# Moving three pieces of work in a hand-ordered attention slot: O's codes on ScalarE, the attention rest and the lower half of Q's weights on VectorE

## The chip, the cores and the metric

The kernel runs on one core of a Trainium2 chip. The metric is the device time of one execution in microseconds (us), lower is better. TensorE does the matrix products, VectorE, ScalarE and GpSimd the rest, and the SyncE queue issues most of the transfers. Every engine works its instructions off in the order in which the program gives them to it, and they meet at semaphores only.

## The reference

One decoder layer in float32 with x of shape (2, 512, 1024):

```python
# 1. self attention, 4-bit weights: (codes - 8) * scale of each 128 rows
h = layernorm(x); q, k, v = h @ Wq, h @ Wk, h @ Wv     # 32 query heads, 8 key/value heads of 128
q, k = rope(q), rope(k)
attn = softmax(q @ k.T / sqrt(128) + causal mask)
x = x + (attn @ v) @ Wo
# 2. cross product with quantised operands
x = x + fake_quant(layernorm(x)) @ fake_quant(ctx)
# 3. dense layer with binarised weights
x = x + layernorm(x) @ binarize(weight).T
```

## The kernel before

The work on attention is cut into 64 **slots**, one for each pair of a query head and a batch element (p = 0 to 63, the batch element b is p mod 2, so even slots are batch 0 and odd ones batch 1). Eight slots make a group (one key/value head for both batch elements). Group 0 is written out, groups 1 to 4 (slots 8 to 39) are a loop of the hardware, in which each slot also prepares a piece of ctx on ScalarE and GpSimd, and groups 5 to 7 are written out again. In slots 0 to 6 and from 41 on the slots also turn pieces of the dense weight.

Each engine has its own list of a slot's work, written by hand (functions `slot`):

- **TensorE**, slot p: `scores(p,0)` (L839 to L841), the last unit of the O product of the slot before, `o_unit(p-1,3)` (L876), `scores(p,1)`, `o_unit(p,0)`, one eighth of the Q projection for slot p+2 (`q_part`, L699 to L701), `scores(p,2)`, more of Q, `o_unit(p,1)`, the rest of Q, `o_unit(p,2)`, and `weigh(p-1)` (L856), attention times V of the slot before, into the PSUM bank `pv_ps`.
- **ScalarE**, slot p: the exponentials of the three score units (`exps`, L1195), the upper half of q (L1187), `q_cut` (L1106), `prob_split(p,0)` (L1222), the two halves of the swap for RoPE (`q_swap`, L1111 and L1112), `ao_part(p-1)` (L1231, the upper half of attention's output, out of `pv_ps`), `prob_split(p,1)` and `o_cut` (L1208, O's codes from int32 to float16). In the loop the parts of ctx stand between (L1289, L1301, L1316) and one load is issued (L1276).
- **VectorE**, slot p: in odd slots a small copy of O's scales (`o_scales`, L1976), `maxima(p,0)` (L1966), `q_sum(p+1)` (L1895, RoPE's last sum), the O add of unit 3 of the slot before (`o_add`, L1990), `maxima(p,1)`, `o_add(p,0)`, `maxima(p,2)`, reciprocals (L2063, L2067) with `piece_scale` (L1722) between them, `piece_lo` (L1728, the lower half of Q's weights), `o_add(p,1)`, `o_add(p,2)`, `q_cos` (L1885) and `ao_rest(p-1)` (L2006, the lower half of attention's output, out of `pv_ps`).
- **GpSimd**, slot p: the lower half of q (L1541), the normalisation (L1527), the clip of ctx (L1635), the lower half of the probabilities (L1534), and between its two parts `sine` (L1522), which `q_sum` waits for.

Waits that matter here: `scores(p,2)` waits for the first exponentials of its slot, which wait for `maxima(p,0)`. The first Q eighth of a slot waits for `q_sum`. And `o_unit` has this wait, in which `cb` is 0 in odd slots and 4 in even ones (`unit_of`):

```python
if k == 0:
    pe.wait_ge(o_codes_done, p - 2)
    if cb == 0:
        pe.wait_ge(ao_ready, p - 1)
```

`ao_ready` counts the `ao_rest` that are done, so that an odd slot's first O unit needs `ao_rest(0)` to `ao_rest(p-2)`.

Of the kernel before, what the change touches and what calls it, by code (L numbers as in the profile page):

```python
# [51 lines left out]
SLOTS = B * RF  # L52
# [70 lines left out]
def wf_late(p):  # L123

    if p < KB:
        return p
    return p - WF_FROM + KB - 1 if p > WF_FROM else None


def wf_early(p):  # L130

    if p < KB:
        return p + 1 if p + 1 < KB else None
    return p - WF_FROM + KB if p >= WF_FROM else None
# [67 lines left out]
def build(nc, x_in, ctx_in, codes, scales, q_scales, q_scalars, ffn_w, rope_cos, rope_sin, ident_in, mask_in, out):  # L202
    with ExitStack() as ctx:
# [303 lines left out]
        def known(n):  # L507
            return isinstance(n, int)
# [580 lines left out]
        def _(act):  # L1089
# [126 lines left out]
            def prob_split(p, part):  # L1216

                act.wait_ge(norm_done, p * 2 + (part + 1))
                if part == 0 and not (known(p) and p == 0):
                    act.wait_ge(prob_turned, p * TURNED)  # L1220
                for at, to, w in prob_runs(part):
                    ins = act.activation(prob16[:, 0, to:to + w], prob[:, at:at + w], ACT.Copy)  # L1222
                ins.then_inc(prob_hi[part], 1)
# [25 lines left out]
            def wf_sign(u):  # L1249

                raw, diff = wf_place(u)
                act.wait_ge(wf_clipped, u + 1)
                if u >= 2:
                    act.wait_ge(wf_split, u)
                act.activation(diff, raw, ACT.Sign).then_inc(wf_signed, 1)
# [8 lines left out]
            def slot(g, i, with_ctx=False):  # L1264
                p = g * SLOTS + i
                has_prev = not (known(p) and p == 0)
                has_next = not (known(p) and p >= N_SLOTS - 1)
                has_ahead = not (known(p) and p >= N_SLOTS - Q_AHEAD)
                has_piece = not (known(p) and p + FIRST_PIECES >= N_CUT)

                if with_ctx:
                    q, dst = ctx_half(g, i)

                    tile = ctx_rows[bass.ds((g - 1) * 4 + i // 2, 1), :, (i % 2) * S:(i % 2 + 1) * S]
                    act.wait_ge(ctx_free, q + 1)
                    act.dma_start(ctx_raw[:, :], tile.rearrange("a p n -> (a p) n")).then_inc(ctx_landed, 16)  # L1276
                if known(p) and p == 1:
                    late_swaps()
                if known(p) and p == 2:
                    late_upper()  # L1280
                exps(p, i, 0)
                if has_next:
                    q_hi(p + 1)
                exps(p, i, 1)
                if known(p) and wf_late(p) is not None:
                    wf_upper(wf_late(p))
                if with_ctx:
                    act.wait_ge(ctx_landed, q * 16 + 16)
                    act.activation(ctx_raw[:, :], ctx_raw[:, :], ACT.Identity, scale=scal[:, 5:6],  # L1289
                                   bias=scal[:, 3:4]).then_inc(ctx_scaled, 1)  # L1290
                exps(p, i, 2)
                if has_piece:
                    q_cut(p, i)
                if known(p) and 0 < p < O_LAG:
                    v_evict(V_HERE + p - 1)
                if known(p) and wf_early(p) is not None:
                    wf_sign(wf_early(p))
                prob_split(p, 0)
                if with_ctx:
                    act.wait_ge(ctx_clipped, q + 1)  # L1300
                    act.activation(ctx_raw[:, :], ctx_raw[:, :], ACT.Copy, bias=ROUND).then_inc(ctx_rounded, 1)  # L1301
                if has_ahead:
                    q_swap(p + Q_AHEAD)
                if known(p) and p == N_SLOTS - 1:
                    prob_split(p, 1)
                    o_cut(p, i)
                    column_part(0, 0)
                    ao_part(p - 1, i - 1)
                    return
                if has_prev:  # L1310
                    ao_part(p - 1, (i - 1) % SLOTS)
                prob_split(p, 1)
                o_cut(p, i)
                if with_ctx:
                    act.wait_ge(ctx_rounded, q + 1)
                    act.activation(dst, ctx_raw[:, :], ACT.Copy, bias=-(ROUND + Q_MID)).then_inc(ctx_free, 1)  # L1316
# [364 lines left out]
        def _(dve):  # L1681
# [234 lines left out]
            def wf_lower(u):  # L1916

                dve.wait_ge(wf_hi, u + 1)
                dve.scalar_tensor_tensor(wf_halves[:, 1, :], wf_place(u)[1], F_UP, wf_halves[:, 0, :],
                                         ALU.mult, ALU.subtract).then_inc(wf_split, 1)  # L1920
# [89 lines left out]
            def slot(g, i):  # L2010
                p = g * SLOTS + i
                has_prev = not (known(p) and p == 0)
                has_next = not (known(p) and p >= N_SLOTS - 1)
                has_ahead = not (known(p) and p >= N_SLOTS - Q_AHEAD)
                has_o = not (known(p) and p < O_LAG)
                has_piece = not (known(p) and p + FIRST_PIECES >= N_CUT)
                n = p + FIRST_PIECES

                if known(p) and p == N_SLOTS - 1:
                    j = o_scales(g, i)  # L2020
                    maxima(p, i, 0)
                    o_add(p - 1, i - 1, 3)
                    maxima(p, i, 1)
                    dve.wait_ge(o_now_ready, j)
                    o_add(p, i, 0)
                    maxima(p, i, 2)
                    dve.wait_ge(exp_done, p * 3 + 2)
                    dve.reciprocal(row_inv[:, 0:3], row_sum[:, 0:3]).then_inc(inv_ready[0], 1)
                    dve.wait_ge(exp_done, p * 3 + 3)
                    dve.reciprocal(row_inv[:, 3:4], row_sum[:, 3:4]).then_inc(inv_ready[1], 1)  # L2030
                    wf_lower(wf_late(p))
                    j = o_scales(g, i, NH)
                    o_add(p, i, 1)
                    wf_difference(wf_early(p))
                    o_add(p, i, 2)
                    o_add(p, i, 3)
                    ao_rest(p - 1, i - 1)
                    for k in range(UNITS):
                        o_add(N_SLOTS, 0, k)
                    dve.wait_ge(o_now_ready, j)  # L2040
                    return
                if has_o and i % B:
                    j = o_scales(g, i)
                if i or known(p):
                    maxima(p, i, 0)
                if known(p) and p == 0:
                    wf_difference(0)
                if has_next:
                    q_sum(p + 1)
                if not (i or known(p)):  # L2050
                    maxima(p, i, 0)
                if has_o and not (known(p) and p == O_LAG):
                    o_add(p - 1, (i - 1) % SLOTS, 3)
                maxima(p, i, 1)
                if has_o:
                    if i % B:
                        dve.wait_ge(o_now_ready, j)
                    o_add(p, i, 0)
                maxima(p, i, 2)
                if known(p) and p < 3:  # L2060
                    (late_join, late_sum, late_lower)[p]()
                dve.wait_ge(exp_done, p * 3 + 2)
                dve.reciprocal(row_inv[:, 0:3], row_sum[:, 0:3]).then_inc(inv_ready[0], 1)  # L2063
                if has_piece:
                    piece_scale(n, i % 2)
                dve.wait_ge(exp_done, p * 3 + 3)
                dve.reciprocal(row_inv[:, 3:4], row_sum[:, 3:4]).then_inc(inv_ready[1], 1)  # L2067
                if known(p) and wf_late(p) is not None:
                    wf_lower(wf_late(p))
                if has_piece:  # L2070
                    piece_lo(n, i % 2, q_region(i), Q_UP)
                if has_o:
                    o_add(p, i, 1)
                if known(p) and wf_early(p) is not None:
                    wf_difference(wf_early(p))
                if has_o:
                    o_add(p, i, 2)
                if known(p) and 0 < p < O_LAG:
                    v_rest(V_HERE + p - 1)
                if has_ahead:  # L2080
                    q_cos(p + Q_AHEAD)
                if has_prev:
                    ao_rest(p - 1, (i - 1) % SLOTS)

            def body(g, with_ctx=False):
                for i in range(SLOTS):
# [186 lines left out]
```

## Time and profile before

| what | value |
|---|---|
| time, median of 3 runs | 1104.35 us (1102.6 to 1105.29) |
| span of the profiled execution, first to last instruction | 1104.9 us |
| granted TensorE clock, mean | 0.992 |
| TensorE busy | 1056.7 us, 96% |
| VectorE busy | 934.1 us, 85% |
| ScalarE busy | 690.9 us, 63% |
| GpSimd busy | 689.6 us, 62% |

The profile is one execution. Times of rows are microseconds from the start of its span. No other device time is given for the profiled execution; its span is 0.55 us above the median of the runs. "PEld" is TensorE's loading of weights, which runs beside its products.

### The profile page before, as it was taken

The page shows a single profiled execution, that of the slowest core. Times are in us where ns is not written, and L with a number is a line of the kernel's source. Part 1 is how long each engine was busy: PE and PEld are TensorE (multiplying, and loading weights), DVE is VectorE, ACT ScalarE, POOL GpSimd, SP SyncE. Part 2 cuts the span into 40 slices and gives each one's busy share as a digit, 9 for nine tenths or more (in the row PEclk, how much of TensorE's full clock was granted, in tenths as well). Part 3 has the DMA queues.
Part 4 walks back from the last instruction along what each step waited for, and adds up shares of the span by engine and source line. Part 5 has one row for each costly group of instructions (what it writes and reads, how often), then busy time and mean ns, then how long its engine had stood idle before and what let it go on. Part 6 is the DMA issues. An engine that isn't in the chain of part 4 may idle for free.

```text
span 1104.9 us, 18938 instructions
## 1 busy us (share of the span) xinstructions
PE 1056.7 (96%) x5448; PEld 513.8 (47%) x5448; DVE 934.1 (85%) x1755; ACT 690.9 (63%) x1502; POOL 689.6 (62%) x770
## 2 busy tenths in 40 slices
PE   3898999899999999999999999999999999989998
PEld 2443444444544444444444444544544544444443
DVE  7977897799888888888888889999999998888873
ACT  4455665766777777777777776666666666463320
POOL 2457546877767766776777677777878777332200
PEclk9999999999999999999999999999999999999999
DMA  9344231767678667657766765777777675432453
GB/s 350 123 135 132 67 101 44 150 149 170 142 155 160 145 147 159 159 134 154 163 148 141 159 160 130 148 155 162 151 150 171 142 128 119 108 117 53 101 103 79
DMA packets 301204, 153.65 MB, mean 139 GB/s; under 512 B 249264, under 2 KB 261808, under 8 KB 301136
## 3 DMA queue, kind: packets, MB, share of 16 engines
q1 hardware_dynamic: 293360, 139.46, 55.3%
q10 hardware_dynamic: 7776, 13.37, 4.4%
q8 instruction: 32, 0.52, 0.2%
q14 instruction: 36, 0.29, 0.1%
HBM read 89.07 MB, written 4.19 MB: 84 GB/s over the span
## 4 chain that ended last, share of the span: by engine, by line
PE 78%; DVE 8%; ACT 5%; POOL 3%; issue 3%; ACTq 1%; DMA 1%; SPq 1%; DVEq 0%; POOLq 0%
PE side_ps L699 10%; PE side_ps L856 9%; PE side_ps L701 9%; PE side_ps L700 9%; PE proj_ps L876 8%; PE out_ps L876 8%; PE proj_ps L1027 4%; PE score_ps L839 3%; PE score_ps L841 2%; PE score_ps L840 2%; PE proj_ps L1032 2%; PE score_ps L998 2%; PE out_ps L719 2%; PE score_ps L719 2%; PE proj_ps L699 2%
## 5 line engine op out<-in xcount | busy, mean ns | idle before, releaser
L1534 POOL TENSOR_TENSOR w_b<-prob,w_b 128x896 f16<-128x896 f32 (+2 forms) x192 | 188.9, 998 | 30.6 <-ACT w_b L1222 30.0
L699 PE MATMUL side_ps<-hT,w_a 128*128 128x512 f16 x504 | 191.1, 379 | 1.5 <-DVE rot L1895 1.5
L701 PE MATMUL side_ps<-hT,w_a 128*128 128x512 f16 x504 | 191.0, 379 | 0.0
L700 PE MATMUL side_ps<-hT,w_a 128*128 128x512 f16 x504 | 191.0, 379 | 0.0
L1990 DVE SCALAR_TENSOR_TENSOR x_acc<-proj_ps,o_now,x_acc 128x1024 f32<-128x1024 f32 x120 | 153.6, 1280 | 37.8 <-PE proj_ps L876 37.8
L1527 POOL TENSOR_SCALAR prob<-prob,row_inv 128x512 f32<-128x512 f32 (+3 forms) x256 | 170.7, 681 | 22.6 <-DVE row_inv L2063 16.9
L1195 ACT ACTIVATE prob<-score_ps,neg_max 128x512 f32<-128x512 f32 (+3 forms) x256 | 132.9, 521 | 47.4 <-DVE neg_max L1966 38.6
L1541 POOL TENSOR_TENSOR q_sb<-rot,q_sb 128x512 f16<-128x512 f32 x64 | 75.0, 1172 | 139.8 <-ACT q_sb L1187 139.8
L1990 DVE SCALAR_TENSOR_TENSOR x_acc<-out_ps,o_now,x_acc 128x1024 f32<-128x1024 f32 x120 | 152.7, 1272 | 0.0
L876 PE MATMUL proj_ps<-work,w_b 128*128 128x512 f16 x496 | 127.3, 379 | 1.9 <-DVE x_acc L1990 1.1
L876 PE MATMUL out_ps<-work,w_b 128*128 128x512 f16 x496 | 127.3, 379 | 1.3 <-DVE x_acc L1990 1.2
L1966 DVE CUSTOM_DVE_ANT_0 score_ps<-score_ps,mask_b 128x512 f32<-128x512 f32 (+3 forms) x256 | 122.1, 497 | 2.0 <-PE score_ps L841 2.0
L1222 ACT ACTIVATE w_b<-prob 128x896 f16<-128x896 f32 (+2 forms) x192 | 99.5, 553 | 34.2 <-POOL prob L1527 30.2
L856 PE MATMUL side_ps<-work,v_sb 128*128 128x512 f16 (+3 forms) x768 | 116.0, 301 | 1.3 <-DMA work<-w_b 1.3
L1522 POOL TENSOR_TENSOR swapped<-swapped,sin_t 128x512 f32<-128x512 f32 x79 | 101.8, 1288 | 22.0 <-ACT swapped L1112 21.8
L856 PEld LDWEIGHTS side_ps<-work,v_sb 128*128 128x128 f16 (+1 forms) x768 | 70.2, 99 | 46.6 <-DMA work<-w_b 1.8
L1231 ACT ACTIVATE work<-side_ps 128x512 f16<-128x512 f32 x64 | 38.2, 597 | 73.1 <-PE side_ps L856 73.0
L839 PE MATMUL score_ps<-k_sb,q_sb 128*128 (+4 forms) x256 | 77.2, 302 | 3.3 <-ACT prob L1195 2.1
L699 PEld LDWEIGHTS side_ps<-hT,w_a 128*128 128x128 f16 x504 | 49.2, 98 | 65.5 <-issue 10.6
L1187 ACT ACTIVATE q_sb<-rot 128x512 f16<-128x512 f32 x64 | 40.3, 630 | 58.9 <-PE score_ps L841 57.6
L701 PEld LDWEIGHTS side_ps<-hT,w_a 128*128 128x128 f16 x504 | 49.3, 98 | 59.5
L840 PE MATMUL score_ps<-k_sb,q_sb 128*128 (+4 forms) x256 | 76.8, 300 | 0.0
(238 smaller groups left out, 2102.5 us busy)
## 6 DMA issues: line engine op xcount, KB each, us to landing
stage_c<-in_codes_dram SPq DMA_DIRECT2D x80, 256.0 KB, 2.9
stage_o<-in_codes_dram SPq DMA_DIRECT2D x64, 256.0 KB, 3.9
stage_s<-in_scales_dram SPq DMA_DIRECT2D x64, 256.0 KB, 3.8
ctx_raw<-in_ctx_dram ACTq DMA_DIRECT2D x32, 256.0 KB, 3.2
work<-w_b SPq DMA_TRANSPOSE x261, 3.0
x_acc<-in_x_dram SPq DMA_DIRECT2D x8, 512.0 KB, 8.5
k_sb<-in_codes_dram SPq DMA_DIRECT2D x16, 256.0 KB, 6.4
v_sb<-in_scales_dram SPq DMA_DIRECT2D x16, 256.0 KB, 7.3
```

Of the source, the lines that this page charges most:

```text
L699: pe.matmul(o, stat(0), mov(0), start=first, stop=False)
L700: pe.matmul(o, stat(0), mov(1), start=False, stop=False)
L701: return pe.matmul(o, stat(1), mov(0), start=False, stop=last)
L839: pe.matmul(o, q[0], k[0], start=True, stop=False)
L856: mm = pe.matmul(pv_ps[:, kb * P:S], v_sb[:, bass.ds(g, 1), l, b * TB + kb, :].rearrange("p a d -> p (a d)"), probT[:, m, at:kb + (TB - 1) ...
L876: mm = pe.matmul(o[:, b, :], o_codes[:, h % RING, cb * P:(cb + 1) * P], ao[:, h % 2, l, b * S:(b + 1) * S], start=l == 0, stop=l == 1)
L1195: ins = act.activation(prob[:, SCORE_AT[qb]:SCORE_AT[qb] + w], score_ps[:, score_bank(i, u), off:off + w], ACT.Exp, bias=neg_max[:, c:c + ...
L1522: pool.tensor_tensor(swapped[:, :], swapped[:, :], sin_t[:, :], ALU.mult).then_inc(done, 1)
L1527: return pool.tensor_scalar(prob[:, at:at + w], prob[:, at:at + w], row_inv[:, col:col + 1], P_UP, ALU.mult, ALU.mult)
L1534: ins = pool.tensor_tensor(prob16[:, 1, to:to + w], prob[:, at:at + w], prob16[:, 0, to:to + w], ALU.subtract)
L1966: ins = dve.tensor_tensor_reduce(s, s, mask_b[:, S - w:S], -1.0, MAX_FROM, ALU.add, ALU.min, neg_max[:, c:c + 1])
L1990: ins = dve.scalar_tensor_tensor(y, u, s, y, ALU.mult, ALU.add)
```

## The change

On ScalarE `o_cut` moves from behind `prob_split(p,1)` to ahead of `prob_split(p,0)`. On VectorE `ao_rest(p-1)` leaves the end of slot p and stands in slot p+1, behind `maxima(p+1,0)` and `q_sum(p+2)` and ahead of the first O add. `piece_lo` moves from ahead of `o_add(p,1)` to behind it. Nothing is added or taken away, and the lists of TensorE, GpSimd and SyncE are the same.

```diff
@@ ScalarE, slot
                     wf_sign(wf_early(p))
+                o_cut(p, i)
                 prob_split(p, 0)
...
                 prob_split(p, 1)
-                o_cut(p, i)
@@ VectorE, slot
+                has_before = not (known(p) and p < 2)
                 if known(p) and p == N_SLOTS - 1:
                     j = o_scales(g, i)
                     maxima(p, i, 0)
+                    ao_rest(p - 2, i - 2)
                     o_add(p - 1, i - 1, 3)
...
                 if not (i or known(p)):
                     maxima(p, i, 0)
+                if has_before:
+                    ao_rest(p - 2, (i - 2) % SLOTS)
                 if has_o and not (known(p) and p == O_LAG):
                     o_add(p - 1, (i - 1) % SLOTS, 3)
...
+                if has_o:
+                    o_add(p, i, 1)
                 if has_piece:
                     piece_lo(n, i % 2, q_region(i), Q_UP)
-                if has_o:
-                    o_add(p, i, 1)
...
                     q_cos(p + Q_AHEAD)
-                if has_prev:
-                    ao_rest(p - 1, (i - 1) % SLOTS)
```

## Rows read from the trace of the kernel before

**Rows 1.** The page: busy time by engine, and the chain that ended last.
```profile
PE 1056.7 (96%) x5448; PEld 513.8 (47%) x5448; DVE 934.1 (85%) x1755; ACT 690.9 (63%) x1502; POOL 689.6 (62%) x770
...
PE 78%; DVE 8%; ACT 5%; POOL 3%; issue 3%; ACTq 1%; DMA 1%; SPq 1%; DVEq 0%; POOLq 0%
```

**Rows 2.** Waits from 240 to 980 us: total, times, longest.
```profile
PEld score_ps L839 <- ACT prob L1195: 16.8, 33, 0.9
...
PEld side_ps L699 <- DVE rot L1895: 6.6, 16, 0.5
```

**Rows 3.** Timeline of TensorE, odd slot 37: start, duration, line, operation.
```profile
629.29 0.38 PE L839 MATMUL score_ps<-k_sb,q_sb 128*128 x1
...
629.72 0.38 PE L841 MATMUL score_ps<-k_sb,q_sb 128*128 x1
...
631.46 1.03 PE L876 MATMUL proj_ps<-work,w_b 128*128 128x512 f16 x4
...
633.13 0.28 PE L839 MATMUL score_ps<-k_sb,q_sb 128*128 x1
```

**Rows 4.** Timeline of VectorE, the same stretch.
```profile
630.12 0.69 DVE L2006 SCALAR_TENSOR_TENSOR work<-side_ps,work 128x512 f16<-128x512 f32 x1 [0.36 <-ACT work L1231]
630.73 0.39 DVE L1976 COPY o_now<-work 128x8 f32 x1
631.04 0.68 DVE L1966 CUSTOM_DVE_ANT_0 score_ps<-score_ps,mask_b 128x512 f32<-128x512 f32 x1
...
631.65 0.68 DVE L1895 TENSOR_TENSOR rot<-side_ps,swapped 128x512 f32<-128x512 f32 x1
632.25 1.27 DVE L1990 SCALAR_TENSOR_TENSOR x_acc<-out_ps,o_now,x_acc 128x1024 f32<-128x1024 f32 x1
```

**Rows 5.** Timeline of ScalarE, slots 36 and 37.
```profile
630.49 0.62 ACT L1208 ACTIVATE w_b<-stage_o 128x512 f16<-128x512 int32 x1
...
632.88 0.19 ACT L1195 ACTIVATION_READ_ACCUMULATOR prob<-score_ps,neg_max 128x1 f32 x1
...
637.68 0.95 ACT L1222 ACTIVATE w_b<-prob 128x896 f16<-128x896 f32 x1 [0.57 <-POOL prob L1527]
```

**Rows 6.** Timeline of GpSimd, the same stretch.
```profile
629.03 1.27 POOL L1522 TENSOR_TENSOR swapped<-swapped,sin_t 128x512 f32<-128x512 f32 x1
630.67 0.43 POOL L1534 TENSOR_TENSOR w_b<-prob,w_b 128x128 f16<-128x128 f32 x1 [0.37 <-ACT w_b L1222]
```

**Rows 7.** Timeline of TensorE: starts of the even slots 36 and 38.
```profile
617.12 0.38 PE L839 MATMUL score_ps<-k_sb,q_sb 128*128 x1
...
641.36 0.38 PE L839 MATMUL score_ps<-k_sb,q_sb 128*128 x1
```

**Rows 8.** Timeline: starts of slots 57, 58 and 59, and slot 57's sine.
```profile
869.44 0.38 PE L839 MATMUL score_ps<-k_sb,q_sb 128*128 128x512 f16 x1
...
881.48 0.38 PE L839 MATMUL score_ps<-k_sb,q_sb 128*128 128x512 f16 x1
...
893.38 0.38 PE L839 MATMUL score_ps<-k_sb,q_sb 128*128 128x512 f16 x1
...
869.13 1.27 POOL L1522 TENSOR_TENSOR swapped<-swapped,sin_t 128x512 f32<-128x512 f32 x1
```

**Rows 9.** Timeline of TensorE, VectorE and GpSimd, slot 3.
```profile
218.49 1.02 PE L876 MATMUL proj_ps<-work,w_b 128*128 128x512 f16 x4 [0.84 <-issue]
220.39 0.38 PE L699 MATMUL side_ps<-hT,w_a 128*128 128x512 f16 x1 [0.88 <-DVE rot L1895]
...
218.31 0.74 DVE L1976 COPY o_now<-work 128x8 f32<-128x8 f32 x1
...
217.75 1.27 POOL L1522 TENSOR_TENSOR swapped<-swapped,sin_t 128x512 f32<-128x512 f32 x1
```

**Rows 10.** Timeline of TensorE, slots 1 and 41.
```profile
197.36 0.28 PE L839 MATMUL score_ps<-k_sb,q_sb 128*128 128x256 f16 x1 [1.11 <-ACT prob L1195]
...
681.29 0.38 PE L699 MATMUL side_ps<-hT,w_a 128*128 128x512 f16 x1 [0.62 <-DVE rot L1895]
```

More of the change, by code:

```diff
@@ L1312, in slot @@
                 prob_split(p, 1)
-                o_cut(p, i)
                 if with_ctx:
```

## The prediction

> **What bounds the kernel now.** I read the page first: TensorE is busy for 96% of the span and carries 78% of the chain that ended last [rows 1]. So a change of order can only give back TensorE's gaps, or make new ones. The list of waits says which gaps the attention slots have: the third score unit waits for the first exponentials, and the first eighth of Q waits for RoPE's sum on VectorE [rows 2]. Then I read the timeline of one pair of slots, engine by engine, to see the size. In the loop the even slot 36 takes 12.17 us (617.12 to 629.29) and the odd slot 37 takes 12.07 us (629.29 to 641.36) [rows 3, 7]. Behind the loop an even slot without a gap takes 11.90 us (slot 58) and an odd one 12.04 us (slot 57) [rows 8]. TensorE's list is the same in all of them, so I take 11.90 us as the slot that has no gap. A pair has 0.44 us of gaps in the loop and 0.14 us behind it. These are all that the change can win in the steady part.
>
> **Why the gaps are there.** I count from W, the start of `scores(p,0)`, 629.29 in slot 37. Its last product ends at 630.10 (W+0.81) [rows 3]. The first maximum could start some 0.04 us later; that step between engines is an estimate, from TensorE's 0.06 us behind the exponentials' end below. It starts at 631.04 (W+1.75), because `ao_rest` (630.12) and the copy of the scales (630.73) stand ahead of it [rows 4]. The exponentials follow, their sum is read out by 633.07 (632.88 and 0.19), and TensorE starts the third score unit at 633.13 [rows 3, 5]. ScalarE is late too: it has O's codes at 630.49 (0.62 us) between its splits and the exponentials [rows 5].
>
> **The change, part by part.**
>
> *O's codes ahead of the split.* ScalarE stands idle for 0.57 us ahead of `prob_split(p,0)`, waiting for GpSimd [rows 5]. The 0.62 us of `o_cut` lie in that hole, up to 0.05 us of them perhaps not. Its own waits are long met there: its codes were loaded a slot earlier, and the O units that it waits for are done by `scores(p,1)`. If that cover were gone it would put 0.62 us ahead of the swaps, and they are `q_cos`'s wait. No transfer moves: SyncE sees `o_codes_done` in the next slot. Behind, ScalarE is free about 0.5 us earlier, so in the loop the exponentials end at about 632.57 instead of 633.07, W+3.3; the third score unit wants them at W+3.68 (633.13, W+3.84, less the odd slot's gaps of 0.17 us). That gap closes.
>
> *`piece_lo` behind the second O add.* O add 2 waits for its unit on TensorE after both, so the pair ends as before. `piece_done` comes 1.2 us later, but SyncE reads it only behind the turns of the slot, and TensorE only in the next slot. I cost it at nothing. What covers it is VectorE's wait ahead of O add 2; without that it would be at most the move itself, one O add of 1.27 us [rows 4], and then `q_cos` and the next maximum would be late.
>
> *`ao_rest` behind the next slot's first maximum.* In an even slot nobody wants it soon, and the maximum starts about 0.6 us earlier. The gaps go. In an odd slot TensorE wants it: `o_unit(p,0)` has the wait on `ao_ready` for `ao_rest(p-2)`, which is now in the same slot. The unit starts at 631.46, W+2.17, with `ao_rest` done at 630.81, 0.65 us before [rows 3, 4]. Afterwards VectorE has the maximum, `q_sum` and only then `ao_rest`. From one start to the next these take 0.61 us (631.04 to 631.65) and 0.60 us (631.65 to 632.25), then `ao_rest` takes 0.69 us, and I add 0.05 us until TensorE starts [rows 4]. That is 1.95 us from the maximum's start. With the maximum at W+0.85 TensorE starts its unit at W+2.80 and stands still for 0.63 us. Everything behind it in TensorE's list stands with it: Q's eighth, `scores(p,2)` and, through them, ScalarE's upper half of q. That a wait of this kind is real can be seen in slot 3: there the O unit starts at 218.49, after TensorE stood still for 0.84 us, and VectorE left `ao_rest` for the copy at 218.31 [rows 9].
>
> *The copy of the scales.* It moves up with the maximum, to about W+0.4, and there GpSimd is in its `sine` (629.03 to 630.30) [rows 6]. Two rows say what that does. In slot 37 the copy starts 0.06 us after a GpSimd TENSOR_TENSOR that ends at 631.10, and ends at 631.12 [rows 4, 6]. In slot 3 it starts inside `sine`, which ends at 219.02, takes 0.74 us for 8 elements, and ends at 219.05 [rows 9]. So the copy ends 0.03 us after the GpSimd instruction, and the maximum starts 0.09 us before the copy's end. The Trainium skill (SBUF — State Buffer, "SBUF: two separate sides") has the rule for it: the port pair that VectorE and GpSimd share is an exclusive lock for a whole instruction, whichever starts first. By that rule the copy waits for all of `sine`; if the copy were free, the stall would be the 0.63 us above.
>
> When does `sine` end? In slot 37 at W+1.01. Its chain starts from the reciprocals of the even slot before, and that slot gets 0.27 us shorter on TensorE while GpSimd's work does not: W+1.28, less some 0.03 us by which the reciprocals come earlier, so W+1.25. The maximum then starts at 1.25+0.03-0.09, W+1.19, and the stall is 1.19+1.95-2.17 = 0.97 us. Behind the loop the even slot has no gap to lose: `sine` ends at 870.40, W+0.96 in slot 57 [rows 8], the maximum starts at W+0.90, and the stall is 0.68 us.
>
> **The sum.** In the loop, 16 odd slots by 0.97 us = 15.5 us. Slots 41 to 61, 11 odd ones by 0.68 us = 7.5 us. Slots 5 and 7, 1.4 us. Slot 3: its copy ends at 219.05 as before, the maximum starts at 218.96, `ao_rest` ends 1.90 us later, and the O unit starts at 220.91 and not at 218.49; Q's eighth, which now starts at 220.39, starts at 221.77: 1.4 us more. Slot 1: its third score unit waited 1.11 us for exponentials on ScalarE [rows 10]; `o_cut` is out of that chain, 0.5 us less. The end of slot 63: 0.1 us more, for one `ao_rest` ahead of its O adds. Together 25.4 us. Against it stand the gaps that go: 16 pairs by 0.44 us = 7.0 us, 10 odd slots behind the loop by 0.14 us = 1.4 us and the 0.62 us of slot 41 [rows 10], and 0.3 us in slots 5 and 7: 9.3 us. Net 16.1 us on the profiled execution's span of 1104.9 us, so 1121.0 us; the median of the runs is 0.55 us lower, and I predict 1120.4 us, 1.5% slower.
>
> **The rivals.**
>
> *The copy doesn't wait (or hardly).* The same stall, but 0.63 us each: 29 odd slots give 18.3 us, slot 3 less its copy's wait 0.7 us, less 0.4 and 9.3 us: +9.3 us, 1113.7 us. For it: other copies fell into a short GpSimd instruction, so I have only slot 3 for a long one. Against it: both rows end with the GpSimd instruction to 0.03 us.
>
> *The stall doesn't bite, and the change is faster.* One mechanism: `ao_rest` is done by W+2.1, so that only the gaps go: 1104.35-9.3-0.5 = 1094.6 us. It decides at a stall of 9.8 us over 30 odd slots, 0.33 us each: below that the kernel gets faster. For it: TensorE has other work ahead, 0.65 us of slack. Against it: three VectorE instructions of known length stand between score and `ao_rest`, and even the short count is 0.3 us over that point. *No measurable change* lies around that point, 1101 to 1107.7 us; 0.3% is about what a measurement of this kernel can tell from no change.
>
> *The exponentials stay late.* The maximum comes earlier but ScalarE, with its load and ctx work, does not start them earlier: the even slots of the loop keep 0.27 us, 16 of them 4.3 us, 1124.7 us. The same price would come if `piece_lo`, which reads two SBUF tiles, or `wf_difference` behind it ran into GpSimd's long TENSOR_TENSOR and O add 2 came late. Against it: 0.4 us of room by the count above.
>
> **How the numbers follow.** The forecast has 0.60, the copy that doesn't wait 0.17, the late exponentials 0.07, no change 0.07, and faster 0.09. Slower by over 0.3% is the first three, 0.84. The bounds of the forecast's own stall are 0.63 and 1.1 us in the loop (the copy free, and `sine` 0.1 us later than counted), from 1114 to 1124 us with the rest. For 8 in 10 the range reaches down over the copy's rival and up over the late exponentials: 1109 to 1126 us.
>
> **What would show it.** In odd slots TensorE's first O unit starts behind L2006's end, at about W+3.1 in the loop and W+2.85 behind it, and the list of waits gets a line of some 20 us, L876 on L2006. The copy L1976 ends with L1522. The third score unit waits for exponentials nowhere in the loop, and even slots take 11.90 us, odd ones about 12.87 us. If the copies last 0.16 to 0.39 us and odd slots 12.5 us, the rival of the free copy is right. If odd slots stay below 12.2 us, the wait was hidden and my count from the maximum to `ao_rest` is wrong.

## The result, and the profile after

| | before | after |
|---|---|---|
| time, median (4 runs each) | 1104.82 us (1102.6 to 1105.6) | 1126.85 us (1124.69 to 1127.37) |
| span of the profiled execution | 1104.9 us | 1125.5 us |
| granted TensorE clock, mean | 0.992 | 0.991 |

The ratio is 1.0200, with a 95% interval of 1.0187 to 1.0214: 2.0% slower, 22.0 us between the medians. 1120.4 us was forecast, so the direction and the place were right, and 6.45 us are missing; the time lies 0.85 us above the range.

The page of the kernel after, busy time by engine and the chain that ended last:
```profile
PE 1054.1 (94%) x5448; PEld 519.5 (46%) x5448; DVE 945.9 (84%) x1755; ACT 683.2 (61%) x1502; POOL 680.4 (60%) x770
...
PE 76%; DVE 12%; issue 5%; POOL 3%; ACT 2%; DMA 1%; DVEq 0%; SPq 0%; ACTq 0%; POOLq 0%
```
Against [rows 1] TensorE's work is the same (2.6 us less busy), and its share of the chain fell from 78% to 76%. VectorE's rose from 8% to 12%: more of the chain now runs over VectorE. The waits from 240 to 980 us, total, times and longest:
```profile
ACT q_sb L1187 <- PE score_ps L841: 102.9, 58, 2.5
...
PEld proj_ps L876 <- issue: 31.1, 30, 1.6
PE proj_ps L876 <- DVE work L2005: 15.6, 16, 1.1
...
PE proj_ps L876 <- issue: 10.8, 14, 1.5
```
The third score unit's wait for the exponentials [rows 2] is no longer among the long ones. In its place TensorE waits at the O unit: 16 times for VectorE's L2005, `ao_rest`, in the loop's 16 odd slots, and 14 times "issue" (no releaser found) in those of the written-out groups, 26.4 us together. ScalarE's wait for `scores(p,2)` ahead of the upper half of q doubled, from 51.8 to 102.9 us; it stands behind the same stall, as forecast.

The odd slot 37, where W is 640.46. TensorE (the first product of each kind), then VectorE, then GpSimd (start, duration, line, operation, idle time before):
```profile
640.46 0.38 PE L839 MATMUL score_ps<-k_sb,q_sb 128*128 x1
...
642.57 0.22 PE L841 MATMUL score_ps<-k_sb,q_sb 128*128 x1
643.73 1.03 PE L876 MATMUL proj_ps<-work,w_b 128*128 128x512 f16 x4 [0.95 <-DVE work L2005]
...
645.25 0.27 PE L839 MATMUL score_ps<-k_sb,q_sb 128*128 x1
...
653.47 0.38 PE L839 MATMUL score_ps<-k_sb,q_sb 128*128 x1
```
```profile
640.83 0.86 DVE L1975 COPY o_now<-work 128x8 f32 x1
641.60 0.69 DVE L1965 CUSTOM_DVE_ANT_0 score_ps<-score_ps,mask_b 128x512 f32<-128x512 f32 x1
...
642.21 0.68 DVE L1894 TENSOR_TENSOR rot<-side_ps,swapped 128x512 f32<-128x512 f32 x1
642.82 0.67 DVE L2005 SCALAR_TENSOR_TENSOR work<-side_ps,work 128x512 f16<-128x512 f32 x1
643.41 1.27 DVE L1989 SCALAR_TENSOR_TENSOR x_acc<-out_ps,o_now,x_acc 128x1024 f32<-128x1024 f32 x1
```
```profile
638.55 1.88 POOL L1533 TENSOR_TENSOR w_b<-prob,w_b 128x896 f16<-128x896 f32 x1
640.40 1.26 POOL L1521 TENSOR_TENSOR swapped<-swapped,sin_t 128x512 f32<-128x512 f32 x1
```
The stall can be followed from right to left. The O unit, at W+2.17 before [rows 3], starts at W+3.27, 0.24 us after `ao_rest` ends (643.49). Ahead of `ao_rest` stand the sum and the maximum, 0.61 us each. The maximum starts at W+1.14, 0.09 us before the end of a copy of 8 elements that takes 0.86 us and ends 0.03 us after `sine`. The third score unit follows without a wait, and the next slot starts after 13.01 us instead of 12.07.

Behind the loop, slot 57 (W 887.76), TensorE, VectorE and GpSimd:
```profile
890.76 0.81 PE L876 MATMUL proj_ps<-work,w_b 128*128 128x512 f16 x3 [0.68 <-issue]
```
```profile
888.13 0.73 DVE L1975 COPY o_now<-work 128x8 f32<-128x8 f32 x1
888.77 0.69 DVE L1965 CUSTOM_DVE_ANT_0 score_ps<-score_ps,mask_b 128x512 f32<-128x512 f32 x1
...
889.99 0.67 DVE L2005 SCALAR_TENSOR_TENSOR work<-side_ps,work 128x512 f16<-128x512 f32 x1
```
```profile
887.56 1.27 POOL L1521 TENSOR_TENSOR swapped<-swapped,sin_t 128x512 f32<-128x512 f32 x1
```
`sine` ends at W+1.07, the maximum starts at W+1.01, and the step from `ao_rest`'s end (890.66) to TensorE is 0.10 us. The O unit is at W+3.00.

In ScalarE's list of slot 37 the second edit shows:
```profile
649.05 0.62 ACT L1208 ACTIVATE w_b<-stage_o 128x512 f16<-128x512 int32 x1
649.67 0.95 ACT L1222 ACTIVATE w_b<-prob 128x896 f16<-128x896 f32 x1
```
The split follows `o_cut` with no idle time; the hole of 0.57 us [rows 5] is filled.

The span in stretches, from one start of `scores(p,0)` to another (us), each worked out as a difference of two starts in TensorE's timeline (the first and the last from the span's start and to its end):

| stretch | before | after | difference | forecast |
|---|---|---|---|---|
| up to slot 0 | 181.87 | 180.88 | -1.0 | 0 |
| slots 0 to 2 | 34.32 | 33.80 | -0.5 | -0.5 |
| slot 3 | 13.06 | 15.50 | +2.4 | +1.4 |
| slots 4 to 7 | 47.87 | 49.25 | +1.4 | +1.1 |
| slots 8 to 39 | 388.47 | 398.98 | +10.5 | +8.5 |
| slots 40 to 61 | 263.76 | 271.33 | +7.6 | +5.5 |
| from slot 62 on | 175.55 | 175.76 | +0.2 | +0.1 |
| span | 1104.9 | 1125.5 | +20.6 | +16.1 |

In the loop even slots went from 12.19 to 11.90 us and odd ones from 12.09 to 13.04 (means of 16).

### The profile page after: what moved, and what is told of

The parts are those of the page before. It is cut to its first block, busy times and chain, and to the rows that moved or that the text cites. A ratio compares the mean times of both kernels' runs of the same rounds, so it can differ in the third digit from the quotient of the medians.

```text
span 1125.5 us, 18942 instructions
## 1 busy us (share of the span) xinstructions
PE 1054.1 (94%) x5448; PEld 519.5 (46%) x5448; DVE 945.9 (84%) x1755; ACT 683.2 (61%) x1502; POOL 680.4 (60%) x770
## 4 chain that ended last, share of the span: by engine, by line
PE 76%; DVE 12%; issue 5%; POOL 3%; ACT 2%; DMA 1%; DVEq 0%; SPq 0%; ACTq 0%; POOLq 0%
PE proj_ps L876 10%; PE side_ps L701 9%; PE side_ps L700 9%; PE side_ps L699 9%; PE out_ps L876 8%; PE side_ps L856 7%; PE proj_ps L1027 4%; PE score_ps L839 2%; PE score_ps L841 2%; PE score_ps L840 2%; PE proj_ps L1032 2%; PE score_ps L998 2%; PE proj_ps L699 1%; PE proj_ps L700 1%; PE proj_ps L701 1%
## 5 line engine op out<-in xcount | busy, mean ns | idle before, releaser
L1526 POOL TENSOR_SCALAR prob<-prob,row_inv 128x512 f32<-128x512 f32 (+3 forms) x256 | 170.4, 678 | 19.4 <-DVE row_inv L2066 12.8
L876 PEld LDWEIGHTS proj_ps<-work,w_b 128*128 128x128 f16 x496 | 44.8, 98 | 80.0 <-issue 34.6
L701 PEld LDWEIGHTS side_ps<-hT,w_a 128*128 128x128 f16 x504 | 49.4, 98 | 59.6 <-issue 0.3
```

The costliest lines, as they stand in the source:

```text
L701: return pe.matmul(o, stat(1), mov(0), start=False, stop=last)
L876: mm = pe.matmul(o[:, b, :], o_codes[:, h % RING, cb * P:(cb + 1) * P], ao[:, h % 2, l, b * S:(b + 1) * S], start=l == 0, stop=l == 1)
L1526: return pool.tensor_scalar(prob[:, at:at + w], prob[:, at:at + w], row_inv[:, col:col + 1], P_UP, ALU.mult, ALU.mult)
```

## The experiments

All times are medians, with lowest and highest. The kernel before was run beside them, 9 times with e1 to e4 and 13 times with e5 to e8, and has 1104.68 us both times. Lengths of slots are from one profiled execution of each kernel.

### e1: the attention rest alone

`ao_rest` moved; `o_cut` and `piece_lo` where they were.
```diff
-                o_cut(p, i)                 # ScalarE, ahead of prob_split(p, 0)
...
                 prob_split(p, 1)
+                o_cut(p, i)
...
+                    piece_lo(n, i % 2, q_region(i), Q_UP)
                 if has_o:
                     o_add(p, i, 1)
-                if has_piece:
-                    piece_lo(n, i % 2, q_region(i), Q_UP)
```
Expected: 

> Only the attention rest moves; O's codes and the lower half of Q's weights stay where they were. My theory (the odd slot's first O unit waits for the attention rest): all of the loss is here, and the loop's even slots keep their 0.27 us gap because ScalarE still has O's codes ahead of the exponentials, 16 x 0.27 = 4.3 us and 0.5 us in slot 1 more than the whole change: about 1131.5 us, odd slots of the loop near 13.0 us, even ones 12.1 to 12.2 us. Rival (the loss comes from the other two moves running into GpSimd or the swaps): near 1105 us.

Measured: 1128.18 us (1126.17 to 1130.21), ratio 1.0215 (1.0201 to 1.0229). This one move is the whole loss. The even slots kept their 12.19 us; the list of waits has what is left of the late exponentials, and the timeline of slot 37 (W 640.95) has a shorter hold:
```profile
PEld score_ps L839 <- ACT prob L1195: 9.5, 15, 0.9
```
```profile
641.32 0.67 DVE L1976 COPY o_now<-work 128x8 f32 x1
641.90 0.70 DVE L1966 CUSTOM_DVE_ANT_0 score_ps<-score_ps,mask_b 128x512 f32<-128x512 f32 x1
```
The even slot before is not shortened, so `sine` ends at W+1.01 as in [rows 6] and the maximum starts at W+0.95: odd slots take 12.87 us in the mean, 0.17 us less than in the kernel after. The expectation had them near 13.0 us; 16 slots by 0.17 us are 2.7 of the 3.3 us by which the time lies below it. And the even slots show that an earlier first maximum alone closes nothing: in slot 36 it starts at W+0.96 instead of W+1.52, and the exponentials at W+3.11 as before.

### e2 and e8: the other two moves, and one of them alone

e2 is the kernel before with `o_cut` and `piece_lo` moved, e8 has `o_cut` alone; `ao_rest` stays at the end of the slot.
```diff
+                o_cut(p, i)                 # e2 and e8
                 prob_split(p, 0)
...
+                if has_piece:               # e2 alone
+                    piece_lo(n, i % 2, q_region(i), Q_UP)
```
Expected, e2: 

> The other two moves without that of the attention rest. My theory: the gaps in front of the third score unit in the loop were ScalarE's, so they go (0.27 us in even and 0.10 us in odd slots, 16 pairs: 5.9 us) and 0.5 us in slot 1: about 1098.5 us. Rival (the maximum behind the attention rest makes those gaps, as the waits of before read): only slot 1's 0.5 us, about 1104 us. Rival (these moves cost): above 1106 us.

Expected, e8: 

> Before with O's codes ahead of the split and nothing else. My theory (the lower half of Q's weights behind the O add is worth nothing either way): the same as the two moves together, 1098.7 us. Rival (that move brings a part of the gain): 1100 to 1104 us.

Measured: e2 1098.74 us (1097.15 to 1100.05), ratio 0.9946 (0.9932 to 0.9960); e8 1098.24 us (1097.12 to 1099.63), ratio 0.9946 (0.9933 to 0.9960). Both are 6 us faster than before, though VectorE still has `ao_rest` and the copy ahead of the maximum. In e8 the loop's slots fell from 12.19 and 12.09 to 11.92 and 11.99 us. VectorE and ScalarE of e8 in slot 37 (W 622.27), then its line in the list of waits from 240 to 980 us:
```profile
624.01 0.69 DVE L1965 CUSTOM_DVE_ANT_0 score_ps<-score_ps,mask_b 128x512 f32<-128x512 f32 x1
```
```profile
624.79 0.69 ACT L1195 ACTIVATE prob<-score_ps,neg_max 128x512 f32<-128x512 f32 x1 [0.71 <-DVE neg_max L1965]
```
```profile
PEld score_ps L839 <- ACT prob L1195: 3.0, 9, 0.5
```
The maximum starts at W+1.74, where it was before (W+1.75), and the exponentials at W+2.52. Before they started at W+3.01:
```profile
632.30 0.69 ACT L1195 ACTIVATE prob<-score_ps,neg_max 128x512 f32<-128x512 f32 x1 [0.67 <-DVE neg_max L1966]
```
They come 0.49 us earlier with the maximum in its place, and the third score unit's wait for them falls from 16.8 us to 3.0. In the even slot 36 they start at W+2.61 with the maximum at W+1.52, and after, with the maximum at W+0.96, at W+2.61 too. So of the two causes that the prediction gave for the late exponentials, ScalarE's 0.62 us of `o_cut` is the one that cost time. Both times are as expected (1098.5 and 1098.7 us). `piece_lo`'s move shows in one slot: slot 41 takes 12.04 us in e2 and 12.67 in e8 and before. The runs' times can't tell 0.6 us.

### e3: the copy of the scales behind the attention rest

```diff
-                if has_o and i % B:
-                    j = o_scales(g, i)
                 if i or known(p):
                     maxima(p, i, 0)
...
                     ao_rest(p - 2, (i - 2) % SLOTS)
+                if has_o and i % B:
+                    j = o_scales(g, i)
```
Expected: 

> The whole change, but the copy of O's scales stands behind the attention rest instead of ahead of the first maximum. My theory (the copy waits for GpSimd's sine): the first maximum of odd slots starts at W+0.85 us instead of 1.15 (loop), 1.32 (group heads) and 1.02 (written out): 13 x 0.30 + 3 x 0.47 + 12 x 0.17 + 1.5 us in slot 63, about 9 us less than the change: 1118 us. Rival (the copy's length is a coincidence, something else holds the maximum): 1126 to 1127 us, the maximum still at W+1.15.

Measured: 1121.08 us (1120.99 to 1121.34), ratio 1.0148 (1.0132 to 1.0163), 5.8 us below the kernel after. VectorE in slot 37 (W 637.30; `sine` runs from 637.25 to 638.52):
```profile
638.25 0.70 DVE L1965 CUSTOM_DVE_ANT_0 score_ps<-score_ps,mask_b 128x512 f32<-128x512 f32 x1 [0.49 <-PE score_ps L841]
...
638.87 0.69 DVE L1894 TENSOR_TENSOR rot<-side_ps,swapped 128x512 f32<-128x512 f32 x1
639.47 0.68 DVE L2005 SCALAR_TENSOR_TENSOR work<-side_ps,work 128x512 f16<-128x512 f32 x1
640.07 0.16 DVE L1975 COPY o_now<-work 128x8 f32 x1
```
The same copy takes 0.16 us here and 0.86 us inside `sine`, and the maximum, which also runs inside `sine`, is not held. So the hold is the copy's, and it cost about 0.2 us in a typical odd slot of the loop (13.02 to 12.84) and 0.05 us behind it (12.73 to 12.68). It is not the main part: the maximum now waits for TensorE and starts at W+0.95, 0.14 us after the scores' end and not the 0.04 us of the prediction, and the O unit comes at W+3.10 (640.40). The time is 3 us above the expectation of 1118 us. Of the gain on the kernel after, 3.1 us lie in the loop and 0.5 us behind it; the rest lies in the first and the last stretch of the span, where the granted clock of the two profiles differs too (below), so that the 1.5 us expected of slot 63 are not shown.

### e4: the wait for the attention rest as the O unit's last

```diff
                 if k == 0:
                     pe.wait_ge(o_codes_done, p - 2)
-                    if cb == 0:
-                        pe.wait_ge(ao_ready, p - 1)
                 ...
                     pe.wait_ge(o_added, p * UNITS + (k - O_BACK - 1))
+                if k == 0 and cb == 0:
+                    pe.wait_ge(ao_ready, p - 1)
```
Expected: 

> The whole change, with the same waits in the O unit in another order: that for the attention rest comes last. The O unit starts 0.24 us behind the attention rest's end in the loop and 0.11 us in the written-out slots, where I had counted 0.05. My theory (the sequencer still has another wait to work off, in the loop with a register to compute, behind the one that holds it): the step falls to about 0.05 to 0.10 us, 16 x 0.15 + 13 x 0.03 = 2 to 3 us less than the change, about 1124.3 us. Rival (the step is the same whatever wait stands last): no difference, 1126.9 us, step 0.24 us.

Measured: 1125.06 us (1123.98 to 1127.37), ratio 1.0187 (1.0173 to 1.0201). TensorE and VectorE in slot 37 (W 639.43):
```profile
642.61 1.02 PE L876 MATMUL proj_ps<-work,w_b 128*128 128x512 f16 x4 [0.86 <-DVE work L2005]
```
```profile
641.79 0.67 DVE L2005 SCALAR_TENSOR_TENSOR work<-side_ps,work 128x512 f16<-128x512 f32 x1
```
The step from `ao_rest`'s end to TensorE's start is 0.15 us instead of 0.24 in the loop; behind it, it grew from 0.10 to 0.15. Expected were 0.05 to 0.10. So the order of the waits is worth about 0.1 us of the loop's step, which fits the theory that the other wait is worked off after the one that holds TensorE; it is not shown apart from it. The rival of a step that no order changes is out. The loop's 16 slots gain some 1.5 us, the 13 written-out ones lose 0.6, and the medians' 1.8 us are within the runs' scatter. Slot 3 differs too, see below.

### e7: the attention rest between the maximum and the sum

The whole change, with `ao_rest` one place further forward (in the first slot of a loop group it stays behind the maximum, which comes after the sum there).
```diff
                     maxima(p, i, 0)
+                    if has_before:
+                        ao_rest(p - 2, (i - 2) % SLOTS)
...
                     q_sum(p + 1)
                 if not (i or known(p)):
                     maxima(p, i, 0)
-                if has_before:
                     ao_rest(p - 2, (i - 2) % SLOTS)
```
Expected: 

> The whole change, with the attention rest directly behind the first maximum and ahead of the RoPE sum (at the head of a group in the loop the order stays). My theory (the O unit's wait is counted along VectorE's list): the stall of each odd slot falls by the sum's 0.60 us, to about 0.5 us in the loop and 0.2 us in the written-out slots, unless Q's eighth then waits for the sum instead (sum done 0.65 us behind the attention rest, one O unit of 0.86 us covers that): 29 x 0.6 = 17 us less than the change, about 1109.5 us. Rival (the stall is tied to ScalarE or to the product on TensorE and not to VectorE's list): 1126 us.

Measured: 1107.48 us (1105.79 to 1108.36), ratio 1.0027 (1.0017 to 1.0037). That is 2.8 us above the kernel before, with its gap in another place. TensorE and VectorE of slot 37 (W 627.63):
```profile
630.31 1.03 PE L876 MATMUL proj_ps<-work,w_b 128*128 128x512 f16 x4 [0.35 <-DVE work L2005]
```
```profile
628.78 0.69 DVE L1965 CUSTOM_DVE_ANT_0 score_ps<-score_ps,mask_b 128x512 f32<-128x512 f32 x1
...
629.39 0.68 DVE L2005 SCALAR_TENSOR_TENSOR work<-side_ps,work 128x512 f16<-128x512 f32 x1
629.99 0.68 DVE L1894 TENSOR_TENSOR rot<-side_ps,swapped 128x512 f32<-128x512 f32 x1
```
Taking the sum's 0.60 us out from ahead of `ao_rest` took 0.60 us from the loop's odd slots (13.04 to 12.44) and from those behind it (12.77 to 12.17), 19.4 us in all by the medians (17 were expected). In slot 3 it took 2.8 us (15.50 to 12.71), and some 1.5 of them are the clock that had fallen there in the profile of after (below). So in the kernel after every 0.1 us ahead of `ao_rest` is 0.1 us of every odd slot.

### e5 and e6: the move only where nobody waits

In e5 an odd slot's first O unit has its `ao_rest` at the end of the even slot before it, as before the change; in even slots the rest stays behind the maximum. e6 also puts the copy behind `q_sum`.
```diff
-                if has_before:
+                if has_before and i % B == 0:
                     ao_rest(p - 2, (i - 2) % SLOTS)
+                if has_o and i % B:         # e6 alone, and not ahead of the maximum
+                    j = o_scales(g, i)
...
                     q_cos(p + Q_AHEAD)
+                if has_prev and i % B == 0:
+                    ao_rest(p - 1, (i - 1) % SLOTS)
```
Expected, e5: 

> The whole change, but the attention rest alternates: that of an odd slot stands at the end of the even slot behind it (its old place), where the O unit of the next odd slot finds it done; that of an even slot stands behind the first maximum of the next even slot, where nobody waits for it. My theory: no stall in odd slots, no gap in even ones: even slots of the loop 11.90 us, odd ones 11.99 us, written-out odd ones 12.03 us, as with the other two moves alone or up to 0.5 us less: about 1098.3 us. Rival (the new place costs something in itself, not only through the O unit's wait): above 1101 us.

Expected, e6: 

> As the alternating kernel, with the copy of O's scales behind the RoPE sum instead of ahead of the first maximum. My theory: maximum and sum of odd slots come 0.31 us earlier, the odd slots' last gaps (0.09 us in the loop, 0.14 us behind it) go: odd slots 11.90 us everywhere, 16 x 0.09 + 13 x 0.14 = 3 us less than the alternating kernel: about 1095.3 us. Rival (the gaps have another cause): the same time as the alternating kernel.

Measured: e5 1097.37 us (1095.52 to 1098.98), ratio 0.9938 (0.9925 to 0.9952); e6 1093.34 us (1093.13 to 1094.14), ratio 0.9902 (0.9887 to 0.9917). e5 is 0.9 us below its expectation, with 11.90 us in the loop's even slots and 11.96 in its odd ones, so the new place costs nothing in itself. e6 is 11.3 us faster than the kernel before and the fastest of all, 2 us below its expectation. TensorE and VectorE in slot 37 (W 620.01):
```profile
622.17 1.03 PE L876 MATMUL proj_ps<-work,w_b 128*128 128x512 f16 x4
```
```profile
620.84 0.69 DVE L2005 SCALAR_TENSOR_TENSOR work<-side_ps,work 128x512 f16<-128x512 f32 x1 [0.37 <-ACT work L1231]
621.44 0.69 DVE L1965 CUSTOM_DVE_ANT_0 score_ps<-score_ps,mask_b 128x512 f32<-128x512 f32 x1
622.05 0.69 DVE L1894 TENSOR_TENSOR rot<-side_ps,swapped 128x512 f32<-128x512 f32 x1
622.65 0.16 DVE L1975 COPY o_now<-work 128x8 f32 x1
```
The O unit starts at W+2.16 with no idle time, and every slot from 8 to 61 but slot 10 (11.97) takes 11.89 or 11.90 us. That confirms the 11.90 us that the prediction took for a slot without a gap. The 0.39 us of the copy ahead of the maximum were the last of the gap.

## Why the prediction was right or wrong

**The mechanism, right.** The odd slot's first O unit waits for an `ao_rest` that is now in the same slot. e1 has the loss without the other moves, e2 has their gain without the loss, and e7 moves the stall one to one. The rival in which the stall doesn't bite is out.

**The copy that waits for `sine`, right.** In after the copies of all 29 odd slots from 5 to 61 end 0.03 us behind `sine`'s end, whatever is left of it when they start, and e3 shows the copy at 0.16 us elsewhere. Slot 49 shows who waits for whom. In after `sine` started 0.03 us ahead of the copy, in e4 0.07 us behind it:
```profile
789.11 1.26 DVE L1975 COPY o_now<-work 128x8 f32<-128x8 f32 x1
789.08 1.26 POOL L1521 TENSOR_TENSOR swapped<-swapped,sin_t 128x512 f32<-128x512 f32 x1
```
```profile
788.02 0.16 DVE L1975 COPY o_now<-work 128x8 f32<-128x8 f32 x1
788.09 1.27 POOL L1521 TENSOR_TENSOR swapped<-swapped,sin_t 128x512 f32<-128x512 f32 x1
```
The Trainium skill (SBUF — State Buffer, "SBUF: two separate sides") makes the port pair that VectorE and GpSimd share an exclusive lock for a whole instruction, whichever starts first; of VectorE's instructions it names those in a two-port mode or with two SBUF inputs. The copy's 0.86 us in slot 37 agree, and so does the order in slot 49. So the rival of the free copy is out by its mechanism. Its price of 1113.7 us was too low as well: with the copy out of the way e3 still took 1121.08 us.

**The gaps that go, right in size, half wrong in cause.** Even slots came to 11.90 us as forecast, so the rival of the late exponentials is out as well. But e8 gets 6.4 us with `o_cut` alone, while e1, with `ao_rest` moved and `o_cut` in its old place, keeps the even slots at 12.19 us. The prediction named `ao_rest` and the copy first, and laid the even slots' gap to them. What it counted for `o_cut` was right: exponentials that end at W+3.3 (625.57 in e8, W+3.30). The copy matters for the 0.07 us in the loop and 0.13 behind it that e6 took from each odd slot over e5, not for the bulk. `o_cut` in ScalarE's hole cost nothing, and `piece_lo` brought no more than slot 41.

**The sum, short by 4.5 us on the span** (6.45 against the medians). The term of the sum that failed is the odd slot's stall, 0.97 us in the loop and 0.68 behind it; measured are 13.04-11.90 = 1.14 and 12.77-11.90 = 0.88 us, and 1.14 us lie above the 1.1 that the prediction took for the loop's upper bound. The count along VectorE's list was right: 1.90 us from the maximum's start to `ao_rest`'s end, 1.89 in slot 37 (641.60 to 643.49). The stall without the copy's hold was put at 0.63 us, and e3, which has it so, shows 12.84-11.90 = 0.94 in the loop and 12.68-11.90 = 0.78 in most slots behind it: the steps between engines at the two ends of that count were too short. The parts:
- "I add 0.05 us until TensorE starts": 0.24 us in the loop, 0.10 behind. I had taken it from one row of another pair of engines, TensorE's 0.06 us behind ScalarE [rows 3, 5]. The miss is 0.19 us in each of the loop's 16 slots, 3.0 us; part of it is given back by the next line. Of the right pair, with the same wait, the trace of before had a case in slot 3:
```profile
217.70 0.69 DVE L2006 SCALAR_TENSOR_TENSOR work<-side_ps,work 128x512 f16<-128x512 f32 x1
```
  `ao_rest` ends there at 218.39 and the O unit starts at 218.49 [rows 9], 0.10 us, the step behind the loop to the hundredth. Read off, it would have left the loop's 0.24 us still short.
- When `sine` ends: the maximum at W+1.14 and not W+1.19 in a typical loop slot, but later in the first odd slot of three of the four groups (13.18 and 13.19 us for the slot); behind the loop at W+1.01 and not W+0.90, as `sine` ends at W+1.07 and not W+0.96, for a reason that was not looked for. With the step of 0.10 us that makes 0.83 us of stall there; slot 49 alone has 1.36.
- "The first maximum could start some 0.04 us later": 0.14 us (e3). In most slots of after `sine`'s hold covers this, and it costs nothing. This is the larger part of why e3 missed its expectation.
- Slot 3: +2.4 us and not +1.4. The copy was not held there (216.19, 0.16 us, ahead of `sine`), the sum was instead, as it needs `sine`. And TensorE's clock fell, below. In e1 and e4, where it did not, slot 3 takes 13.98 and 14.04 us, +0.9 and +1.0.

The first stretch of the span, up to slot 0, goes with TensorE's granted clock in the first 180 us of the profile: 180.2 to 180.4 us at 0.99 (e1, e3, e5, e7), 180.7 to 181.1 at 0.98 (after, e6, e8) and 181.5 to 182.8 at 0.97 (before, e2, e4). So the 1.0 us by which it is shorter goes with the clock of these two executions, and is no effect of the change that I can show. The account of the span is: 16 times 1.14 and 11 times 0.88 us are 27.9 us, slot 3 has 2.4, slots 5 and 7 together 1.7, the end 0.2, 32.2 us of loss (25.9 forecast, without slot 1). The gaps closed are 7.7 us in the loop (18.2 us of stall less the 10.5 measured), 2.1 behind it, 0.3 in slots 5 and 7 and 0.5 in slot 1, 10.6 us (9.8 forecast with slot 1). With the 1.0 us at the start that is 20.6 us.

The 0.2 us at the end are no test of the 0.1 forecast there. Before, slot 62 took 11.07 us at a granted clock of 0.89, after 8.87 us at 1.00 (e8, with `ao_rest` in its old place, 9.00 at 1.00); from slot 63 on before took 164.5 us at 0.99 and after 166.9 us at 0.97. Two differences of over 2 us nearly cancel, each beside another clock, and what slot 63 costs is not separated from them.

The other 1.9 us of the 6.45 are the step from the span to the median. The prediction took 0.55 us off; the median of after lies 1.35 us above its profile's span. In every recorded run the time is 1.7 to 1.9 us above its own span, so the profiled execution of before took about 1106.8 us by my estimate, some 2 us more than its median. It was a slow one for its kernel, with the clock low in the two stretches just named.

**What stays open.** The step is 0.15 us with the wait last, in the loop and behind it, against 0.10 behind the loop with the wait ahead: why the written-out wait is quicker in the middle was not tried. Nor is it known why `sine` ends 0.11 us later behind the loop.

## What to carry to other kernels

A step moved on one engine must be priced in each parity or phase of the pattern by its earliest reader: here an odd slot's O unit left `ao_rest` 0.65 us of room and an even slot's didn't wait for it at all, so that it could be moved in half of the slots (e6, 1% faster), and moved in all of them the kernel is 2% slower. When several moves are meant to close one gap, run each alone: `o_cut`, on the engine that looked idle, had most of it. And where a count ends in a step between two engines, take that step from a row of the same two engines with the same kind of wait (0.10 to 0.24 us here from VectorE to TensorE), or keep it as a bound. Where a median is worked out from a profile's span, ask first whether that execution was a typical one: a low clock in one slot was worth 2 us here.

## What the runs showed of the hardware

- A VectorE copy of 128x8 takes 0.16 us alone and 0.86 us inside a GpSimd TENSOR_TENSOR, up to 1.26 us when that one has just started (after, slot 49). `o_scales` waits for no semaphore, so here the two engines meet outside the semaphores as well. The maximum, on a PSUM operand, kept its 0.70 us inside `sine` (e3, 638.25).
- While TensorE stood still for 2.80 us ahead of slot 3's O unit, the granted clock fell, and not in e1 in the same stall of 2.79 us. Windows of 214 to 230 us, columns: length, then busy time of each engine, granted clock, DMA share, GB/s. After, then e1:
```profile
218.00:220.00 2.00, 1.05 (x3) 0.43 (x4) 1.62 (x6) 0.00 (x0) 1.59 (x3) 0.66 0.78 155
220.00:226.00 6.00, 6.00 (x26) 2.63 (x25) 3.65 (x8) 2.97 (x10) 2.67 (x3) 0.83 0.72 202
```
```profile
218.00:220.00 2.00, 1.05 (x5) 0.51 (x6) 1.63 (x6) 0.00 (x0) 1.60 (x3) 1.00 0.78 155
220.00:226.00 6.00, 6.00 (x31) 2.87 (x30) 5.06 (x9) 3.98 (x11) 4.17 (x5) 1.00 0.83 211
```
  At the lower of the two levels (1.2 GHz) a product of 512 columns follows the last after 0.43 us (220.61 to 221.04) and not after 0.22 us. e3 fell as well (0.65), e4 did not. It costs some 1.5 us (slot 3 takes 15.50 us in after and 13.98 in e1). What decides between them is open.
